# Dropping a same-engine wait before seven of the operations on VectorE and ScalarE

## What is computed

```python
# x: (2, 8192, 1024); 16 heads of 64, window 256, q = k = v = x
scores = einsum('bhcqd,bhckd->bhcqk', q, k)          # 3 blocks of 256 keys per block of 256 queries
scores = where(|k_pos - q_pos| <= 256 & in range, scores, -1e9)
attn   = einsum('bhcqk,bhckd->bhcqd', softmax(scores), v)
x1 = layernorm(x + attn, g1, b1)
ff = maximum(x1 @ W1 + b1, 0) @ W2 + b2              # 1024 -> 4096 -> 1024
x2 = layernorm(x1 + ff, g2, b2)
u  = layernorm(x + x2)
# 8 experts, top 2 of softmax(u @ Wg.T + bg), renormalized
for e in experts:
    gate, up = split(u @ w1[e].T)                    # 1024 -> 2 x 1024
    acc += combine[:, e] * ((silu(gate) * up) @ w2[e].T)
out = layernorm(u + acc)
```

## Time and profile before

| | us |
|---|---|
| runs | 3428.48 and 3174.91, median 3301.7 |
| profiled execution | 3177.34 |
| its span, slowest core (core 6) | 3175.7 |
| spans of the eight cores | 3163.1 to 3175.7 |
| busy PE / DVE / ACT / POOL | 2299.5 / 967.2 / 511.0 / 148.0 |

### The profile page before, as it was taken

One profiled execution on the slowest core, in us unless ns is written; L12 is line 12 of the kernel. 1 busy time (PEld: TensorE's weight loads), 2 busy tenths in 40 slices (PEclk: granted clock), 3 DMA queues, 4 the chain that ended last, 5 costly groups with the idle time before them and its releaser, 6 DMA issues.

```text
span 3175.7 us, 32348 instructions; the slowest of 8 cores (3163.1 to 3175.7 us)
## 1 busy us (share of the span) xinstructions
PE 2299.5 (72%) x11290; PEld 1081.8 (34%) x11290; DVE 967.2 (30%) x1829; ACT 511.0 (16%) x746; POOL 148.0 (5%) x282
## 2 busy tenths in 40 slices
PE   0366666640698899900369988999889998999880
PEld 0133333320344344400224433444344443444330
DVE  0244444457200230057333311233113321233115
ACT  0133333320031031000011111111111111111110
POOL 1000000000000000000000001000100001000010
PEclk9999999999999999955579999999999999999995
DMA  9400000001044334230012234122332223323232
GB/s 214 82 1 1 1 1 1 1 1 23 16 74 73 60 67 73 54 106 0 1 35 46 42 52 67 37 44 40 58 62 34 47 47 60 53 41 51 43 54 106
DMA packets 49805, 148.21 MB, mean 47 GB/s; under 512 B 4920, under 2 KB 7648, under 8 KB 47600
## 3 DMA queue, kind: packets, MB, share of 16 engines
q0 software_dynamic: 39808, 115.49, 21.3%
q1 hardware_dynamic: 9840, 30.66, 3.2%
HBM read 248.96 MB, written 8.42 MB: 81 GB/s over the span
## 4 chain that ended last, share of the span: by engine, by line
PE 65%; DVE 16%; issue 6%; ACT 5%; SPq 3%; DMA 3%; DVEq 1%; ACTq 0%; POOL 0%; POOLq 0%
PE ob L643 14%; PE hg L579 14%; PE hu L579 13%; PE hb L459 7%; PE hb L430 7%; DVE x0s L128 6%; PE ppv L269 3%; SPq L140 3%; DVE strb L128 3%; DVE bn L128 3%; PE ps L324 2%; ACT osb L132 2%; ACT strb L132 2%; DVE attnh L128 1%; PE ptm L289 1%
## 5 line engine op out<-in xcount | busy, mean ns | idle before, releaser
L579 PE MATMUL hg<-ubf,w1T 128*128 128x512 bf16 x2048 | 486.5, 381 | 16.9 <-DMA w1T<-w1tt 9.0
L579 PE MATMUL hu<-ubf,w1T 128*128 128x512 bf16 x2048 | 484.4, 379 | 0.0
L643 PE MATMUL ob<-a,w2t 128*128 128x512 bf16 x2048 | 452.5, 379 | 9.3 <-DVE a L128 9.3
L128 DVE TENSOR_TENSOR x0s<-pbf,x0s 128x1024 f32<-128x1024 bf16 x80 | 97.9, 1224 | 938.2 <-PE pbf L661 500.9
L128 DVE TENSOR_TENSOR sg<-sg,crep 128x512 bf16<-128x512 bf16 x256 | 108.8, 425 | 597.2 <-ACT sg L132 575.6
L579 PEld LDWEIGHTS hg<-ubf,w1T 128*128 128x128 bf16 x2048 | 200.3, 98 | 260.7 <-issue 22.2
L579 PEld LDWEIGHTS hu<-ubf,w1T 128*128 128x128 bf16 x2048 | 200.7, 98 | 242.7 <-issue 1.9
L643 PEld LDWEIGHTS ob<-a,w2t 128*128 128x128 bf16 x2048 | 197.6, 98 | 237.7 <-issue 11.2
L132 ACT ACTIVATE sg<-hg 128x512 bf16<-128x512 f32 x256 | 152.9, 597 | 742.5 <-PE hu L579 742.5
L132 ACT ACTIVATE strb<-ps 128x640 bf16<-128x640 f32 (+4 forms) x320 | 191.2, 597 | 376.1 <-PE ps L324 371.4
L269 PE MATMUL ppv<-strb,x0tm 128*65 128x128 bf16 x1280 | 185.8, 309 | 80.0 <-DVE strb L128 80.0
(11 more groups left out here) (64 smaller groups left out, 956.5 us busy)
## 6 DMA issues: line engine op xcount, KB each, us to landing
w1T<-w1tt POOLq DMA_DIRECT2D x64, 512.0 KB, 5.1
w2t<-w2tt POOLq DMA_DIRECT2D x128, 256.0 KB, 4.6
w1buf<-W1p POOLq DMA_DIRECT2D x32, 512.0 KB, 5.9
w2buf<-W2p POOLq DMA_DIRECT2D x16, 1024.0 KB, 9.3
x0s<-x SPq DMA_DIRECT2D x1, 8192.0 KB
x0r<-x SPq DMA_DIRECT2D x1, 8192.0 KB, 28.6
out<-x0s SPq DMA_DIRECT2D x1, 8192.0 KB, 25.0
x0tm<-x0p POOLq DMA_DIRECT2D x20, 260.0 KB, 40.4
```

What stands on the lines that cost most here:

```text
L128: return self.vmark(getattr(self.nc.vector, name)(*args, **kw))
L579: ins = nc.tensor.matmul(hps[:], bass.AP(self.w1T, slot2 * 2048 + kc * 256 + hu * 128, [[2 * 2048, 128], [1, 128]]), self.ubf[:, kc, 512 * ...
L643: ins = nc.tensor.matmul(self.ob[:, 512 * nb:512 * nb + 512], self.w2t[:, dsl, eidx, 128 * jc:128 * jc + 128], self.a[:, eidx, jc, 1024 * ...
```

## The change

Two helpers are added, `vop_nw` and `sop_nw`, which issue and mark an operation without the wait for the engine's own latest one. They take the place of `vop` and `sop` at these operations:

- attention: the copy to attnh, the reciprocal, the four scalar_tensor_tensor, the exponential, the mask product
- feed-forward: the relu, the eviction with bias
- experts: the silu

Two explicit waits on DVE's own semaphore are added: ahead of the reciprocal one for the last scalar_tensor_tensor of the group before, which read invz, and behind it one for the reciprocal itself, ahead of the four operations that read invz. Waits on other engines' semaphores stay. All other DVE and ACT operations keep their self-wait.

```diff
--- before.py
+++ after.py
@@ -127,8 +127,14 @@
         self.wait("vector", self.sV, self.cV)
         return self.vmark(getattr(self.nc.vector, name)(*args, **kw))
 
+    def vop_nw(self, name, *args, **kw):
+        return self.vmark(getattr(self.nc.vector, name)(*args, **kw))
+
     def sop(self, name, *args, **kw):
         self.wait("scalar", self.sS, self.cS)
+        return self.smark(getattr(self.nc.scalar, name)(*args, **kw))
+
+    def sop_nw(self, name, *args, **kw):
         return self.smark(getattr(self.nc.scalar, name)(*args, **kw))
 
     def qdma(self, out, in_):
@@ -279,7 +285,7 @@
                 self.wait("vector", self.sT, pv_mark[gb])
                 if gg >= 2:
                     self.wait("vector", self.sT, trans_mark.get(gg - 2, 0))
-                evac_mark[gb] = self.vop(
+                evac_mark[gb] = self.vop_nw(
                     "tensor_copy", self.attnh[0:65, gg % 2, :], ppv[0:65, :])
                 self.wait("tensor", self.sV, evac_mark[gb])
                 if gg >= 2:
@@ -292,11 +298,13 @@
                         self.idf[0:65, 0:65])
                 trans_mark[gg] = self.tmark(ins)
                 self.wait("vector", self.sT, trans_mark[gg])
-                self.vop("reciprocal", self.invz[:, 0:4],
-                         bass.AP(ptm, 64, [[512, 128], [65, 4]]))
+                self.wait("vector", self.sV, stt_mark.get(gg - 1, 0))
+                rm = self.vop_nw("reciprocal", self.invz[:, 0:4],
+                                 bass.AP(ptm, 64, [[512, 128], [65, 4]]))
+                self.wait("vector", self.sV, rm)
                 for tl in range(4):
                     T2 = 4 * grp + tl
-                    ins = self.vop(
+                    ins = self.vop_nw(
                         "scalar_tensor_tensor",
                         self.x0s[:, T2, 64 * h:64 * h + 64],
                         ptm[:, 65 * tl:65 * tl + 64],
@@ -330,13 +338,13 @@
                 self.wait("scalar", self.sT, qk_m)
                 if gidx >= RING:
                     self.wait("scalar", self.sT, strip_last_pv.get(gidx - RING, 0))
-                exp_mark[gidx] = self.sop(
+                exp_mark[gidx] = self.sop_nw(
                     "activation", self.strb[:, slot, 0:w], ps[:, 0:w],
                     AF.Exp, bias=-SHIFT, scale=1.0)
                 self.wait("vector", self.sS, exp_mark[gidx])
                 if gidx >= RING:
                     self.wait("vector", self.sT, strip_last_pv.get(gidx - RING, 0))
-                mask_mark[gidx] = self.vop(
+                mask_mark[gidx] = self.vop_nw(
                     "tensor_mul", self.strb[:, slot, 0:w],
                     self.strb[:, slot, 0:w], self.msk[:, m, 0:w])
                 T = m - LAG
@@ -435,7 +443,7 @@
                                 start=(ki == 0), stop=(ki == FC - 1))
                     mmk = self.tmark(ins)
                     self.wait("scalar", self.sT, mmk)
-                    relu_mark[mig_g] = self.sop("activation", 
+                    relu_mark[mig_g] = self.sop_nw("activation", 
                         self.hsb[:, mig, :], hb[:, 0:1024], AF.Relu,
                         bias=self.b1s[:, mig:mig + 1], scale=1.0)
                     mig_g += 1
@@ -466,7 +474,7 @@
                 self.wait("scalar", self.sT, mmk)
                 if dc_g >= 2:
                     self.wait("scalar", self.sT, flip_mark[dc_g - 2])
-                ev2_mark[dc_g] = self.sop("activation", 
+                ev2_mark[dc_g] = self.sop_nw("activation", 
                     self.ffsb[:, dslot, :], fb[:, 0:1024], AF.Identity,
                     bias=self.b2c[:, dc:dc + 1], scale=1.0)
                 self.wait("tensor", self.sS, ev2_mark[dc_g])
@@ -588,7 +596,7 @@
                 self.wait("scalar", self.sT, hm)
                 self.wait("scalar", self.sV,
                           amul_mark.get((e, g, tq - 2), amul_mark.get(("prevu", qsl), 0)))
-                sm = self.sop("activation",
+                sm = self.sop_nw("activation",
                     self.sg[:, qsl, :], self.hg[qsl][:], AF.Silu,
                     bias=0.0, scale=1.0)
                 silu_mark[(e, g, tq)] = sm
```

## The result

The changed kernel takes 0.9834 of the time before, with a 95% interval of 0.9823 to 0.9845: the medians are 3123.5 us against 3175.6, 52 us less. Forecast were 3130, and a change within 2%, which is what came. Some executions of every kernel here show a lower granted clock on some cores and take longer; all times and ratios in this text are those of the others.

The account below looks back on a forecast made before the run. Attention was taken to run on latency, the experts on PE. Savings of 2.91 us a head, 46.6 for sixteen, plus 1.2 outside attention make 47.8 off 3177.34: say 3130 us, range 3114 to 3163.

Parts of the forecast that it names:

- Where the kernel is bound: Attention, 118 to 689 us, runs on latency with no engine the bound; the experts' stage is a plain PE bound.
- rivals 3 and 4: Whole kernel: 3, nothing changes, 3177 us, chance 0.06; 4, slower through PE's clock, 3210 at 80 us, chance 0.03.
- Issue price: Each removed wait on the path saves its issue time after a late release: 0.055 us on ACT, 0.07 on DVE.
- the head boundary: Start of a head's first group: three exponentials in series and one mask save 3 x 0.055 + 0.07 = 0.235 us.
- The gap of neighbours: Back-to-back DVE operations: the 0.105 us gap becomes -0.05, so a neighbour pair saves 0.155 us.
- inner: Attention's inner group, twice per head: 0.45 to the mask, 0.125 for a link, 0.155 for the copy; 0.73 us saved.
- last: Last group of a head: 0.62 for four pairs, 0.125 for one link, 0.07 for the copy; 0.81 us saved.
- first: Head boundary with first group: 0.235, two links 0.25, and the copy 0.155; 0.64 us saved.
- a third of the fixed part: DVE neighbours: a third of an operation's 0.158 us fixed time overlaps, giving the -0.05 gap taken.
- The bound by exp A: Inner group: the mask after four scalar_tensor_tensor also needs its exponential, so no more than 0.47 us; 0.45 taken.
- Rival 2: DVE neighbours in attention: gaps stay, only the issue price is saved, 0.93 us a head; 3161 us, chance 0.12.
- Outside attention: Feed-forward bias eviction 0.9 us, relu 0.1, silu at the ends of expert pairs 0.2; sum 1.2 us saved.

Follow-up runs that it names:

- the norms' kernel: Changed kernel plus staggered layer norms over three statistics buffers, and no self-wait on the experts' second eviction and 16 additions of x; 0.9638 of before.

## Why the prediction was right

**Where the kernel is bound.** Right. Attention ran on latency, all stages behind it kept their length, and PE was granted the same clock in each of them (1.00 in attention and in the experts' stage, 0.50 in the stretch of the second norm), so rivals 3 and 4 are out. From attention's first score matmul to the end of its last scalar_tensor_tensor, core 6 took 573.8 us and now takes 522.6, 51.1 less, where 46.6 were forecast.

**Issue price, 0.055 and 0.07 us.** Right. ACT's 0.055 is shown three ways: taken away alone, put back satisfied, and with three more added. DVE's 0.07 was never changed by itself; it is read from masks that start 0.10, 0.17 and 0.24 us behind their exp with one, two and three waits. The price is paid per instruction behind a late release, satisfied or not. The prediction used it in the right number of places, apart from one count that only shows when exps are changed alone, the head boundary, where two paths ran level.

**The gap of neighbours.** The mechanism was right, and this is the term whose size was off. Taken was -0.05 us, a pair saving 0.155; measured is -0.08 for scalar_tensor_tensor (0.187 for the first pair, 0.196 for each of the others) and -0.08 between mask and copy (0.18). With these numbers in the prediction's own sums:

| group | working | sum | measured |
|---|---|---|---|
| inner | 0.47 + 0.125 + 0.18 | 0.78 | 0.78 |
| last | 0.187 + 3 x 0.196 + 0.125 + 0.07 | 0.97 | 0.98 |
| first | 0.235 + 0.25 + 0.18 | 0.67 | 0.67 |

A head then gives 3.2 us and sixteen give 51 us, the whole of what attention lost. The sizes are read from the changed kernel's own trace, so the table bears out the count of links and pairs, not the sizes. The last group was furthest off (0.81 for 0.98), because it alone has four pairs with nothing that bounds them. Choosing a third of the fixed part was a guess between bounds, and that the total came within 5 us of the measured gain is in part luck: the overlap is about half of the 0.158 us.

**The bound by exp A.** Right: 0.47 was the most an inner group could have, and mask A now starts 0.10 behind exp A. Without this bound the four pairs, at their measured sizes, would have been counted at 0.78.

**The rule against the change.** Rival 2, the gaps stay, gave 3161 and is refuted: scalar_tensor_tensor operations start every 0.192 us without a wait, and two statistics of the norms' kernel span 1.23 us in place of 1.49. The Trainium skill, VectorE: DVE Perf Modes, section "The DRAIN you can't avoid", says that leaving the semaphores out saves nothing; where each operation had waited for the one before, as here, that doesn't hold: 0.388 us from start to start became 0.192. The section "Two Vector instructions with no wait between them" of the same page of the Trainium skill, by which only a held instruction waits until all earlier ones have finished, agrees with these rows.

**Outside attention.** The forecast of 1.2 us can be seen only at its largest part, 0.9 us of waits. No run here can tell the rest.

## What to carry to other kernels

A self-wait ahead of each operation has two prices: an instruction's issue time behind every late release, even if it is already satisfied (0.055 us on ACT, 0.07 on DVE here), and the lost overlap of back-to-back neighbours (0.2 us a pair on DVE here). Count the first along the path of one period of the loop, and the second only up to the next operand that arrives late. Where operations depend on each other, wait for the one that made the operand and stagger the loop so that it isn't the latest; and check in the same pass that cross-engine waits name the buffer that is being reused: two stages in which one didn't were worth about 78 us here, more than all self-waits of attention.

## What the runs showed of the hardware that was not expected

- A satisfied wait between two VectorE operations doesn't separate them: four scalar_tensor_tensor span 0.86 us with it and without it, and the copy starts 0.41 us after the mask's start either way.
- VectorE overlap holds for long operations as well: two statistics over 512 columns in 1.23 us instead of 1.49, each recorded at about 0.66.
- ScalarE's operations overlap too: the pair of 640-column exps at a head's start spans 1.30 us, 0.11 less than two times 0.704, where it was 1.50 before. On this path it gained nothing, as the second of the pair had slack.
